# An attention layer in slots of 128 tokens: maxima transposed into the value bank, the latents' softmax normalised behind its product, and the projected queries and keys copied by ScalarE

## The chip, the cores and the metric

The kernel runs on one core of a Trainium2 chip. The metric is the device time of one execution in microseconds. A core has five engines that run their own instruction streams in order and wait for each other by semaphores: TensorE (PE; its weight loads are PEld), VectorE (DVE), ScalarE (ACT), GpSimd (POOL) and SyncE (SP), which here only issues DMA transfers.

## What is computed

The input is x of 4 x 1024 x 256, with a condition of 4 x 256 that gives scales, shifts and gates for each batch. Cut to what matters here:

```
h = layernorm(x) * (1 + scale) + shift
q, k, v = h @ qkv_w                       # 16 heads of 16
local  = softmax(q k^T / 4, keys of the last 128 tokens) @ v
pooled = mean of h over chunks of 16 tokens        # 64 latents
rq = h @ rq_w;  rk, rv = pooled @ rkv_w            # 4 heads of 16
lattn = softmax(rq rk^T / 4, latents of earlier chunks); 0 where there are none
remote = (lattn @ rv) @ rout_w
gate = sigmoid(local @ gl_w + remote @ gr_w)
x1 = x + gated((gate * local + (1 - gate) * remote) @ out_w)
out = a second and a third layernorm of x1, added to x1 by the condition
```

The latents' part is the one whose softmax is changed: for each token and each of 4 heads the exponentials of up to 64 scores, divided by their sum, times the values `rv`.

## The kernel before

The 4096 tokens are 32 tiles of 128 tokens (8 to a batch). Every engine has its program written by hand, as a loop over slots: `slot(t, stages)` does for several tiles one stage each. In slot t the tile t+4 is normalised and transposed, t+3 is projected to queries and keys (`project_half`), t+2 has its queries and keys split into three bf16 terms (`part1`, `res1`, `part2`, `part3`) that SP stores to DRAM and loads again as stacks, t+1 gets its values and latents, t its local scores and their maxima, t-1 its exponentials and their sums with the values, t-2 its gate, mix and output projection, t-3 its last norms. The order in which an engine's `slot` calls its functions is the order on that engine; nothing is reordered afterwards. Semaphores named `..._ready`, `..._psum` or `..._copied` count tiles.

Eight PSUM banks hold everything PE writes, and several stages share each: p_qkv takes the queries and keys of `project_half`, the values of `project_v`, the remote part and the transposed maxima of `max_t`; p_misc takes the latents' product (`lat_out_t`), the transposed outputs (`out_tokens`), the mix and the output projection; p_pv takes the sums of probabilities with values (`sum_v`); p_a takes the transposed input and all of the latents' scores.

The steps of a slot that matter:

- ScalarE's `out_t` copies p_pv to `oT` after the last `sum_v` of the slot before. PE's `max_t` transposes the negated maxima; ScalarE's `shift` spreads them over the heads as 16 extra rows of the stacked queries. Then PE's `scores_t` makes the scores with keys on the partitions, two heads at a time into one of two banks, ScalarE's `exps` takes them out, POOL's `mask` clears what lies outside the window (four heads at a time), and `sum_v` uses them.
- The latents: `lat_scores` (PE), `lat_max` (VectorE), `lat_exp` (ScalarE, four exponentials, each with a sum over the row by the accumulator), `lat_recip` and `lat_norm` (VectorE: `lrec` and `lp`), `lat_p_t` (PE transposes `lp`), `lat_pT` (ScalarE copies it), and in the next slot `lat_out_t` (PE: product with the values spread by head, `bvd`), `lat_oT` (ScalarE copies it to `loT`) and `lat_remote` (PE).
- VectorE's `local_out` makes `local` from `out_tokens`, and POOL's `difference` makes `dif` from it. On POOL a slot is `res1`, `rstd1`, `part3`, `add_u`, `add_bias`, `difference`, `rstd2_of`, three masks, `rstd3_of`, the last mask.
- SP stores the terms of a tile after `part3`; for the odd tile of a pair (its keys) it loads the stack right after that store has landed, in three transfers, and the first scores of the next slot wait for it.

## Time and profile before

| | before |
|---|---|
| median of 3 runs | 580.47 us (572.05, 580.47, 580.49) |
| profiled execution | 576.64 us, span 574.9 us |
| busy, share of the span | PE 482.9 us (84%), VectorE 436.6 (76%), POOL 379.2 (66%), ScalarE 353.8 (62%) |
| weight loads on PE | 364.1 us (63%) |
| mean granted TensorE clock | 0.949 of full |

The span is the time from the first to the last instruction of the profiled execution. Busy times are sums over an engine's instructions. Matmuls overlap each other in the array and their ends are modelled, so a busy PE is not a PE without waits. In rows of the timeline a start, a length, the engine, the line of the kernel and the operation with its output and input stand in that order; in brackets is the idle time of the engine just before, and what ended it.

### The profile page before, as it was taken

To read this page: it belongs to the slowest core of one execution; us is meant where nothing else is said; L and a number is where in the kernel's file an instruction comes from. 1 tells how busy PE (TensorE), PEld (TensorE's weight loads), DVE (VectorE), ACT (ScalarE), POOL (GpSimd) and SP (SyncE) were. 2 spreads that over 40 slices of the span, in tenths; PEclk is the share of its full clock that TensorE was granted. 3 is DMA by queue.
4 is the path that set the end of the run, shared out by engine and by line. 5 is a ranking of instruction groups with operands and counts; after the bars stand their busy time and mean duration, and the time that the engine had idled before them with its cause. 6 is when DMAs were issued, how large, how long until landed. Compare 5 with 4: busy or idle time off the path is not lost.

```text
span 574.9 us, 19855 instructions
## 1 busy us (share of the span) xinstructions
PE 482.9 (84%) x7168; PEld 364.1 (63%) x7168; DVE 436.6 (76%) x1193; ACT 353.8 (62%) x868; POOL 379.2 (66%) x516
## 2 busy tenths in 40 slices
PE   2446689999899999999999999999999999988771
PEld 2205567777677666777777676777776676766451
DVE  2155657788688888988988788888888887878554
ACT  1210466677677667777777577777776776766540
POOL 2222346778577767788877587777777677766663
PEclk9975889999899999999999899999999999999776
DMA  9558644618244444434252607162534444440000
GB/s 277 114 133 246 163 105 99 132 47 187 56 113 75 95 94 93 94 90 93 64 101 68 119 34 145 39 125 62 120 68 97 92 94 93 82 79 10 11 10 19
DMA packets 56523, 55.15 MB, mean 96 GB/s; under 512 B 7380, under 2 KB 53100, under 8 KB 54892
## 3 DMA queue, kind: packets, MB, share of 16 engines
q1 hardware_dynamic: 53564, 52.57, 41.4%
q10 hardware_dynamic: 2864, 1.31, 1.1%
q8 instruction: 59, 0.97, 0.8%
q14 instruction: 36, 0.29, 0.2%
HBM read 37.07 MB, written 16.80 MB: 94 GB/s over the span
## 4 chain that ended last, share of the span: by engine, by line
PE 72%; issue 11%; POOL 5%; DVE 4%; DMA 2%; ACT 2%; ACTq 1%; SPq 1%; POOLq 0%; DVEq 0%
PE p_pv L819 9%; PE p_qkv L730 9%; PE p_qkv L740 6%; PE p_misc L886 6%; PE p_y L806 5%; PE p_x L785 5%; PE p_y L807 5%; PE p_x L778 4%; PE p_a L751 3%; PE p_qkv L860 3%; PE p_misc L869 2%; PE p_a L831 2%; PE p_a L716 2%; PE p_misc L877 2%; PE p_a L753 2%
## 5 line engine op out<-in xcount | busy, mean ns | idle before, releaser
L592 ACT ACTIVATE pr<-p_y 128x512 f32<-128x512 f32 x224 | 124.6, 595 | 55.8 <-PE p_y L807 52.9
L1159 DVE TENSOR_REDUCE mtok<-p_x 128x3 bf16<-128x480 f32 (+1 forms) x192 | 109.3, 585 | 30.9 <-PE p_x L785 29.6
L441 POOL TENSOR_SCALAR_AFFINE_SELECT pr<-pr 128x512 f32<-128x512 f32 x128 | 89.6, 701 | 11.2 <-ACT pr L594 9.0
L451 POOL TENSOR_TENSOR rstd<-ve,half 128x1 f32<-128x1 f32 x96 | 58.1, 605 | 47.9 <-DVE ve L1079 47.7
L469 POOL TENSOR_TENSOR dif<-local,rem 128x272 f32<-128x272 f32 x32 | 30.9, 965 | 83.8 <-DVE local L1197 83.8
L445 POOL TENSOR_SCALAR_AFFINE_SELECT pr<-pr 128x512 f32<-128x512 f32 x112 | 81.3, 726 | 0.0
L807 PE MATMUL p_y<-qst,kst 112*128 112x128 bf16 x512 | 73.2, 221 | 0.0
L806 PE MATMUL p_y<-qst,kst 112*128 112x128 bf16 x448 | 66.5, 221 | 7.7 <-ACT pr L592 4.8
L819 PE MATMUL p_pv<-pr,vp 128*18 128x128 f32 x1920 | 67.1, 279 | 2.1 <-POOL pr L445 0.8
L730 PE MATMUL p_qkv<-hT,wqk 128*128 128x256 f32 x256 | 66.1, 403 | 2.2 <-DVE qkf L1111 1.3
L740 PE MATMUL p_qkv<-wv,hT 128*128 128x272 f32 x128 | 40.1, 439 | 29.5 <-issue 29.4
L819 PEld LDWEIGHTS p_pv<-pr,vp 128*18 128x18 f32 x1920 | 48.0, 99 | 19.8 <-POOL pr L445 10.3
L583 ACT ACTIVATE qst<-p_qkv 16x2048 bf16<-16x2048 bf16 x32 | 59.8, 1869 | 0.8
L785 PE MATMUL p_x<-kst,qst 96*32 96x160 bf16 x1792 | 59.3, 235 | 0.5 <-issue 0.5
L600 ACT ACTIVATE oT<-p_pv 128x512 f32<-128x512 f32 x32 | 19.1, 597 | 65.6 <-PE p_pv L819 65.6
L807 PEld LDWEIGHTS p_y<-qst,kst 112*128 112x128 bf16 x512 | 49.0, 99 | 9.7 <-issue 0.9
L730 PEld LDWEIGHTS p_qkv<-hT,wqk 128*128 128x128 f32 x256 | 48.3, 199 | 9.3 <-issue 2.2
L806 PEld LDWEIGHTS p_y<-qst,kst 112*128 112x128 bf16 x448 | 42.8, 98 | 17.5 <-issue 7.9
L425 POOL TENSOR_TENSOR qkf<-qkf,terms 128x512 f32<-128x512 f32 x32 | 40.7, 1271 | 19.5 <-ACT terms L571 19.4
L740 PEld LDWEIGHTS p_qkv<-wv,hT 128*128 128x128 f32 x128 | 23.2, 201 | 37.6 <-issue 34.7
L778 PE MATMUL p_x<-edge,ident_bf 128*32 128x192 bf16 (+1 forms) x672 | 43.5, 249 | 4.0 <-issue 3.9
L432 POOL TENSOR_TENSOR terms<-qkf,terms 128x512 bf16<-128x512 f32 x32 | 37.1, 1160 | 11.7 <-ACT terms L577 11.6
(131 smaller groups left out, 1092.7 us busy)
## 6 DMA issues: line engine op xcount, KB each, us to landing
scr_q<-terms SPq DMA_DIRECT2D x16, 384.0 KB, 2.5
qst<-scr_q SPq DMA_DIRECT2D x16, 384.0 KB, 4.7
scr_k<-terms SPq DMA_DIRECT2D x16, 384.0 KB, 4.4
kst<-scr_k SPq DMA_DIRECT2D x16, 384.0 KB, 5.4
qst<-scr_q SPq DMA_DIRECT2D x16, 256.0 KB, 5.4
kst<-scr_k SPq DMA_DIRECT2D x16, 256.0 KB, 6.4
out_y<-y SPq DMA_DIRECT2D x32, 128.0 KB, 1.7
x_all<-in_x SPq DMA_DIRECT2D x3, 1024.0 KB, 8.3
```

The source lines that it names most:

```text
L441: ins = pool.affine_select(out=own, in_=own, compare_op=ALU.is_ge, fill=0.0, base=-1, pattern=[[0, 4], [1, P]], channel_multiplier=-1)
L445: ins = pool.affine_select(out=prev, in_=prev, compare_op=ALU.is_ge, fill=0.0, base=-1, pattern=[[0, 4], [-P, P]], channel_multiplier=P + 1)
L583: act.activation(q_of(t)[KS:KS + H, :, :], p_qkv[KS:KS + H, 0:P // 2].bitcast(BF16).unsqueeze(1).to_broadcast([H, H, P]), ACT.Copy).then_i ...
L592: act.activation(pr[:, 2 * i:2 * i + 2, :, :], src, ACT.Exp).then_inc(exp_done[i], 1)
L730: ins = pe.matmul(p_qkv[:, 2 * b * P:2 * (b + 1) * P], wqk[:, k, half * D + b * P:half * D + (b + 1) * P], hT[:, r:r + 2, k, :], start=(k ...
L740: ins = pe.matmul(p_qkv[:, 0:H * (HD + 1)], hT[:, t % 4, k, :], wv[:, k, :, :].rearrange("p h k -> p (h k)"), start=(k == 0), stop=(k == K ...
L778: pe.matmul(ends[g * QG:(g + 1) * QG], ident_bf[:, g * QG:(g + 1) * QG], edge[:, :].unsqueeze(1).to_broadcast([P, h1 - h0, 2 * QG]).rearra ...
L785: ins = pe.matmul(win[g * QG:(g + 1) * QG, h - h0, :], q_of(t)[0:KS, h, g * QG:(g + 1) * QG], keys[:, at:at + WIN], start=False, stop=True ...
L806: pe.matmul(p_y[i % 2][:, at:at + P], kst[0:KS + H, h, (n - 1) % NB, :], q, start=True, stop=True)
L807: ins = pe.matmul(p_y[i % 2][:, at + P:at + 2 * P], kst[0:KS + H, h, n % NB, :], q, start=True, stop=True)
L819: ins = pe.matmul(p_pv[32 * j:32 * j + VC, g * P:(g + 1) * P], vp[:, (n - 1 + a) % RING, h, :], pr[:, h, a, :], start=(a == 0 or n % NB == ...
L1159: dve.tensor_reduce(mtok[:, KS + h0:KS + h1], p_x[i % 2][:, 0:(h1 - h0) * w].rearrange("p (h n) -> p h n", n=w), AX_X, ALU.max, negate=Tru ...
```

## The change

Three edits go together.

1. `max_t` writes the transposed maxima into p_pv instead of p_qkv, and `shift` reads them there. So `project_v` waits for the remote part of an earlier tile instead of `shift`, and `max_t` waits for `oT` of the tile before. On PE `scores(t, 1)` is now ahead of `max_t`.
2. The latents' exponentials are transposed and multiplied as they are, without sums by the accumulator. The constant 0/1 pattern of `bvd` stands beside the values, so that the same product gives 64 rows of values and 64 rows of the sums, each repeated for its head's 16 rows. VectorE then takes the reciprocal of the sums (`rden`, 64x128) and multiplies (`loT`); ScalarE's copy `lat_oT` is gone. For the first tile of a batch the 16 tokens without latents are set to 0 from `rden`.
3. `copy_qk` moves from VectorE (one operation of 128x512) to ScalarE (two of 128x256), between the exponentials 4 and 7 of the slot. In ScalarE's slot `out_t` now comes before `part1`, and `shift` before `part2`.

```diff
             def shift(t):
                 act.wait_ge(mT_psum, done(t))
                 act.wait_ge(st_psum[LAST_ST], done(t - 4))
-                act.activation(q_of(t)[KS:KS + H, :, :], p_qkv[KS:KS + H, 0:P // 2].bitcast(BF16).unsqueeze(1).to_broadcast([H, H, P]),
+                act.activation(q_of(t)[KS:KS + H, :, :], p_pv[KS:KS + H, 0:P // 2].bitcast(BF16).unsqueeze(1).to_broadcast([H, H, P]),
                                ACT.Copy).then_inc(shift_ready, 1)
...
+            def copy_qk(t):
+
+                half = t % 2
+                act.wait_ge(qk_psum, done(t))
+                act.wait_ge(part3_ready, done(t - 2))
+                for b in range(KC):
+                    ins = act.activation(qkf[:, half, b, :], p_qkv[:, 2 * b * P:2 * (b + 1) * P], ACT.Identity,
+                                         bias=bqk[:, half, b:b + 1])
+                ins.then_inc(qk_copied, 1)
...
             def project_v(t):
                 pe.wait_ge(hT_ready, done(t))

-                pe.wait_ge(shift_ready, done(t - 2))
+                pe.wait_ge(rem_ready, done(t - 3))
                 pe.wait_ge(qk_copied, done(t + 1))
...
             def max_t(t):
                 pe.wait_ge(s_max[LAST_MAX], done(t))

-                pe.wait_ge(qk_copied, done(t + 3))
-                pe.wait_ge(rem_ready, done(t - 1))
-                pe.transpose(p_qkv[:, 0:P // 2].bitcast(BF16), mtok[:, :], ident_bf[:, :]).then_inc(mT_psum, 1)
+                pe.wait_ge(oT_ready, done(t - 1))
+                pe.transpose(p_pv[:, 0:P // 2].bitcast(BF16), mtok[:, :], ident_bf[:, :]).then_inc(mT_psum, 1)
...
             def lat_exp(t):
                 act.wait_ge(lmx_ready, done(t))
-                act.wait_ge(lp_ready, done(t - 1))
+                act.wait_ge(lpT_psum, done(t - 1))
                 for h in range(LH):
-                    ins = act.activation(by_head(le, t)[:, h, :], by_head(p_a, t)[:, h, :], ACT.Exp, bias=lneg[:, h:h + 1],
-                                         accum_out=lsum[:, h:h + 1])
+                    ins = act.activation(by_head(le, t)[:, h, :], by_head(p_a, t)[:, h, :], ACT.Exp, bias=lneg[:, h:h + 1])
...
-            def lat_oT(t):
-                act.wait_ge(loT_psum, done(t))
-                act.wait_ge(rem_psum, done(t - 1))
-                act.activation(loT[0:LD, :], p_misc[0:LD, 0:P], ACT.Copy).then_inc(loT_ready, 1)
...
             def lat_recip(t):
-                dve.wait_ge(lexp_ready, done(t))
+
+                dve.wait_ge(loT_psum, done(t))
+                dve.reciprocal(rden[:, :], p_misc[LD:2 * LD, 0:P]).then_inc(rden_ready, 1)
+
+            def lat_norm(t):
+
+                dve.wait_ge(rden_ready, done(t))
+                dve.wait_ge(rem_psum, done(t - 1))
                 if t % NB:
-                    dve.reciprocal(lrec[:, :], lsum[:, :]).then_inc(lval_ready, 1)
+                    dve.tensor_tensor(loT[0:LD, :], p_misc[0:LD, 0:P], rden[:, :], ALU.mult).then_inc(loT_ready, 1)
...
```

Where the three edits move rows: on ScalarE, between the end of one slot and the start of the next (`mixT`, `lpT` close a slot; `terms` are `part1` and `part2`, `oT` is `out_t`, `qst` is `shift`), before:

```order
L638 ACTIVATE mixT<-p_misc 128x256 [waits out_psum,mixT_psum]
L615 ACTIVATE lpT<-p_a 128x256 [waits loT_psum,lpT_psum]
L571 ACTIVATE terms<-qkf 128x512 [waits q_terms_stored,qk_copied]
L600 ACTIVATE oT<-p_pv 128x512 [waits o_psum,pv_psum0]
L577 ACTIVATE terms<-qkf 128x512 [waits res_ready]
L583 ACTIVATE qst<-p_qkv 16x16x128 [waits st_psum6,mT_psum]
L620 ACTIVATE loT<-p_misc 64x128 [waits rem_psum,loT_psum]
```

and after:

```order
L642 ACTIVATE mixT<-p_misc 128x256 [waits out_psum,mixT_psum]
L624 ACTIVATE lpT<-p_a 128x256 [waits loT_psum,lpT_psum]
L610 ACTIVATE oT<-p_pv 128x512 [waits o_psum,pv_psum0]
L581 ACTIVATE terms<-qkf 128x512 [waits k_terms_stored,qk_copied]
L593 ACTIVATE qst<-p_pv 16x16x128 [waits st_psum6,mT_psum]
L587 ACTIVATE terms<-qkf 128x512 [waits res_ready]
L617 ACTIVATE le<-p_a,lneg 128x64 [waits lpT_psum,lmx_ready]
```

`part1` went from the end of the slot to behind `oT`, `part2` from ahead of `shift` to behind it, and the copy to `loT` is gone.

On VectorE, from `norm1` (`xn`) to `local` of one slot, before:

```order
L1094 TENSOR_SCALAR xn<-x_all,mv,rstd 128x256 [waits hT_psum,rstd1_ready]
L1159 TENSOR_REDUCE mtok<-p_x 128x3 [waits mT_psum,s_psum3]
L1118 TENSOR_TENSOR vp<-p_qkv,bv 128x16x17 [waits pv_psum0,v_psum]
L1186 TENSOR_SCALAR ssum<-p_misc 128x16 [waits o_psum]
L1064 BN_AGGR mv<-st 128x2 [waits st2_ready]
L1191 RECIPROCAL srec<-ssum 128x16 [waits ssum_ready]
L1079 TENSOR_SCALAR ve<-mv 128x1 [waits mv2_ready]
L1197 TENSOR_TENSOR local<-p_misc,srec 128x272 [waits dif_ready,srec_ready]
```

and after:

```order
L1106 TENSOR_SCALAR xn<-x_all,mv,rstd 128x256 [waits hT_psum,rstd1_ready]
L1175 RECIPROCAL rden<-p_misc 64x128 [waits loT_psum]
L1182 TENSOR_TENSOR loT<-p_misc,rden 64x128 [waits rem_psum,rden_ready]
L1163 TENSOR_REDUCE mtok<-p_x 128x3 [waits mT_psum,s_psum3]
L1122 TENSOR_TENSOR vp<-p_qkv,bv 128x16x17 [waits pv_psum0,v_psum]
L1191 TENSOR_SCALAR ssum<-p_misc 128x16 [waits o_psum]
L1076 BN_AGGR mv<-st 128x2 [waits st2_ready]
L1196 RECIPROCAL srec<-ssum 128x16 [waits ssum_ready]
L1091 TENSOR_SCALAR ve<-mv 128x1 [waits mv2_ready]
L1202 TENSOR_TENSOR local<-p_misc,srec 128x272 [waits dif_ready,srec_ready]
```

The reciprocal `rden` and the product `loT` now stand between `norm1` and the maxima, so ahead of `vp`, `ssum` and `local`.

On PE, at the start of an even slot (the first with a new pair's stacks), before:

```order
L795 MATMUL p_qkv<-ident_bf,mtok 128x128 [waits rem_ready,qk_copied,s_max4]
L778 MATMUL p_x<-edge,ident_bf 32x3x2x32 [waits s_max5,k_stack_loaded,q_stack_loaded]
L778 MATMUL p_x<-edge,ident_bf 32x3x2x32 x3
L785 MATMUL p_x<-kst,qst 32x160 x12
L778 MATMUL p_x<-edge,ident_bf 32x3x2x32 [waits s_max4,k_stack_loaded,q_stack_loaded]
```

and after:

```order
L788 MATMUL p_x<-edge,ident_bf 32x3x2x32 [waits s_max5,k_stack_loaded,q_stack_loaded]
L788 MATMUL p_x<-edge,ident_bf 32x3x2x32 x3
L795 MATMUL p_x<-kst,qst 32x160 x12
L804 MATMUL p_pv<-ident_bf,mtok 128x128 [waits oT_ready,s_max4]
L788 MATMUL p_x<-edge,ident_bf 32x3x2x32 [waits s_max4,k_stack_loaded,q_stack_loaded]
```

The transpose of `mtok` went behind the first scores, into p_pv, and waits for `oT`.

## Rows read from the trace of the kernel before

**Rows 1.** Who waited for whom, 82.1 to 558.4 us (us in total, times, longest)
```profile
POOL dif L469 <- DVE local L1197: 81.8, 31, 5.6
...
PEld p_qkv L740 <- issue: 32.3, 29, 1.4
```

**Rows 2.** The chain that ended last, 280 to 330 us (start, us, what)
```profile
284.15 0.16 PE p_qkv L795
...
285.02 0.63 PE p_a L831 x2
...
288.71 0.44 PE p_misc L869 x4
...
293.35 1.81 PE p_qkv L730 x8
...
298.13 1.44 PE p_pv L819 x48
```

**Rows 3.** Timeline of ScalarE, 269 to 300 us
```profile
284.22 0.60 ACT L600 ACTIVATE oT<-p_pv 128x512 f32<-128x512 f32 x1 [1.85 <-PE p_pv L819]
284.71 0.62 ACT L577 ACTIVATE terms<-qkf 128x512 bf16<-128x512 f32 x1
285.36 1.87 ACT L583 ACTIVATE qst<-p_qkv 16x2048 bf16<-16x2048 bf16 x1
...
295.42 1.09 ACT L592 ACTIVATE pr<-p_y 128x512 f32<-128x512 f32 x2 [1.17 <-PE p_y L807]
...
297.09 0.63 ACT L571 ACTIVATE terms<-qkf 128x512 bf16<-128x512 f32 x1
```

**Rows 4.** Timeline of POOL, 269 to 300 us
```profile
284.58 0.56 POOL L451 TENSOR_TENSOR rstd<-ve,half 128x1 f32<-128x1 f32 x1 [0.78 <-DVE ve L1079]
...
290.21 1.00 POOL L469 TENSOR_TENSOR dif<-local,rem 128x272 f32<-128x272 f32 x1 [2.22 <-DVE local L1197]
...
297.83 1.32 POOL L425 TENSOR_TENSOR qkf<-qkf,terms 128x512 f32<-128x512 f32 x1
```

**Rows 5.** Timeline of VectorE, 269 to 300 us
```profile
286.59 0.82 DVE L1094 TENSOR_SCALAR xn<-x_all,mv,rstd 128x256 f32<-128x256 f32 x1
287.33 0.65 DVE L1159 TENSOR_REDUCE mtok<-p_x 128x3 bf16<-128x480 f32 x1
288.52 0.44 DVE L1118 TENSOR_TENSOR vp<-p_qkv,bv 128x272 f32<-128x272 f32 x1 [0.55 <-PE p_qkv L740]
289.19 0.17 DVE L1186 TENSOR_SCALAR ssum<-p_misc 128x16 f32<-128x16 f32 x1 [0.23 <-PE p_misc L869]
...
289.69 0.44 DVE L1197 TENSOR_TENSOR local<-p_misc,srec 128x272 f32<-128x272 f32 x1
```

**Rows 6.** Line of the oT copies: count, ns, first and last start
```profile
L600 ACT ACTIVATE oT<-p_pv x32: 597/597/597, 82.1 to 558.3; 128x512 f32<-128x512 f32 x32
```

**Rows 7.** Groups by form (count, busy us, mean ns, idle before)
```profile
L638 ACT ACTIVATE mixT<-p_misc 128x256 f32<-128x256 f32 x32 | 12.3, 383 | 8.4 <-PE p_misc L877 7.9
...
L1125 DVE TENSOR_SCALAR rqT<-p_a,brq 64x128 f32<-64x128 f32 x32 | 10.4, 326 | 1.8 <-PE p_a L756 1.8
...
L1191 DVE RECIPROCAL srec<-ssum 128x16 f32<-128x16 f32 x32 | 8.1, 253 | 0.0
...
L1171 DVE RECIPROCAL lrec<-lsum 128x4 f32<-128x4 f32 x28 | 4.7, 168 | 0.0
...
L984 DVE RECIPROCAL cs<-cs 128x8 f32<-128x8 f32 x1 | 0.2, 203 | 0.0
```

**Rows 8.** Timeline of the DMA queue, 284 to 300 us
```profile
286.59 0.38 SPq L350 DMA_DIRECT2D scr_k<-terms  x1
```

**Rows 9.** The line of the stack reloads, 290 to 294 us
```profile
L370 SPq DMA_DIRECT2D kst<-scr_k x3: 557/619/640, 291.3 to 292.6; - x3
...
DMA to landing us min/median/max: 5.4/6.3/6.5
```

**Rows 10.** Busy times of 318 to 322 us; granted clock third from the end
```profile
318.00:322.00 4.00, 4.00 (x31) 2.96 (x32) 1.42 (x8) 1.87 (x11) 0.51 (x1) 0.58 0.40 111
```

More of the change, by code:

```diff
@@ L647, in slot @@
                 if Q:
-                    part2(r)
+                    part1(r)
                 if T:
                     shift(m)
-                    lat_oT(m)
+                if Q:
+                    part2(r)
                 if S:
@@ L667, in slot @@
                     exps(m, 4)
+                if PR:
+                    copy_qk(h)
+                if T:
                     exps(m, 7)
@@ L679, in _ @@
             modulated(b1)
+            copy_qk(b0)
             part1(b0)
+            copy_qk(b1)
             part2(b0)
@@ L850, in lat_out_t @@
                 for k in range(chunks):
-                    ins = pe.matmul(p_misc[:, 0:P], bvd[:, t % 2, k, :], lpT[:, k * P:(k + 1) * P],
+                    ins = pe.matmul(p_misc[:, 0:P], values_of(t)[:, k, :], lpT[:, k * P:(k + 1) * P],
                                     start=(k == 0), stop=(k == chunks - 1))
@@ L893, in slot @@
                 A, PR, K, S, T, C = ("A" in stages, "P" in stages, "K" in stages, "S" in stages, "T" in stages, "C" in stages)
+                if S:
+                    scores(t, 1)
                 if T:
@@ L896, in slot @@
                 if S:
-                    scores(t, 1)
                     scores(t, 0)
@@ L1023, in weights @@
                       dve.memset(loT[LD:LD + 1, :], 1.0),
+                      *[dve.tensor_copy(bvd[:, r, :, LD:2 * LD], cst[:, C_RV:C_RV + 2 * LD].rearrange("p (k l) -> p k l", k=2))
+                        for r in range(2)],
+                      *[dve.tensor_copy(bvd1[:, r, LD:2 * LD], cst[:, C_RV1:C_RV1 + LD]) for r in range(2)],
                       dve.tensor_copy(rqT[LD:P, 0, :], cst[LD:P, C_IND:C_IND + P]),
@@ L1104, in pool_tokens @@
                                   AX_X, ALU.add).then_inc(pooled_ready, 1)
-            def copy_qk(t):
-                half = t % 2
-                dve.wait_ge(qk_psum, done(t))
-                dve.wait_ge(part3_ready, done(t - 2))
-                dve.tensor_tensor(qkf[:, half, :, :], p_qkv[:, :].rearrange("p (b n) -> p b n", b=KC),
-                                  bc(bqk[:, half, :], 2 * P), ALU.add).then_inc(qk_copied, 1)
             def copy_v(t):
@@ L1270, in slot @@
                     norm1(a)
+                if T:
+                    lat_recip(m)
+                    lat_norm(m)
                 if S:
```

55 lines of the change are left out of this document (18 added, 37 removed).

## The prediction

> **What bounds the kernel now.** I began with the table of who waited for whom [rows 1]. Its longest lines have an engine standing still before the same few events of every slot: POOL before `dif`, 81.8 us in 31 slots, and PE before `project_v`, 32.3 us in 29. The second is the wait that this change removes: `project_v` writes p_qkv, and ScalarE's `shift` still reads it. Whether that wait sets the end is a question for the slot, so I next took one full slot and laid its four engines beside each other: PE by the chain that ended last [rows 2], ScalarE [rows 3], POOL [rows 4], VectorE [rows 5]. All times below are of that slot (t = 15), which begins for PE at 284.15 and for the next tile at 299.57; the 32 `oT` copies, 82.1 to 558.3 us [rows 6], give (558.3 - 82.1) / 31 = 15.36 us for a slot.
>
> The reader is to see two things. First, PE's chain of waits looks like a PE bound (nearly every piece of it is a matmul), but the slot closes on POOL. `dif` starts at 290.21, 0.08 after VectorE's `local` ends (289.69 + 0.44), and from there POOL runs without a pause (the ten rows left out there, eight selects in four masks among them, carry no idle time in brackets) to the residual that follows the last mask at 297.83 [rows 4]; PE's last 48 sum matmuls start at 298.13 [rows 2], and their end starts the next slot. So whatever delays `local` delays the slot by the same amount. Second, ScalarE ends the slot nearly as late: its last pair of exponentials starts at 295.42 [rows 3], the moment PE is past `project_half`, and mask 3 follows that pair. Both chains arrive together; neither has room for half a microsecond.
>
> **The change part by part.**
>
> *Maxima in the value bank.* `project_v` no longer waits for `shift`: it gives PE up to 32.3 / 29 = 1.1 us per slot. But the transpose of the maxima now waits for `oT` (284.22 + 0.60 = 284.82 [rows 3]), where it ran at 284.15 [rows 2]; `scores(t, 1)`, put ahead of it, fills 0.4 of that, so 0.3 of idle PE comes back, and `scores(t, 0)`, the latents' scores and their values' product are queued behind it and start 0.3 later than at 285.02 [rows 2]. `shift` itself starts no earlier: ScalarE has `oT` and `part1` in front of it, 0.49 + 0.65, which is again 285.36 [rows 3]. Net for PE alone: a gain of 0.8 per slot at `project_v`.
>
> *ScalarE's new order.* `part1` ran in the idle time before `oT` (297.09 [rows 3]; the residual on POOL started right behind the mask at 297.83 [rows 4]). Now it stands behind `oT`, which waits for the end of the sums. That is no cost to ScalarE, but POOL's next two instructions are the residual `res1` and then the `rstd` that VectorE's `norm1` needs. So: `part1` 284.71 to 285.34, `res1` of 1.32 [rows 4] to 286.74, `rstd` of 0.56 [rows 4] to 287.30, `norm1` at about 287.35, where the trace has it at 286.59 [rows 5]. That is 0.75 late. `part2`, the third term and the store to DRAM move with it; I come back to them.
>
> *Latents normalised behind the product.* VectorE loses a reciprocal of 128x4 (0.17), the product `lp` and, with the next part, the copy of 128x512: more than a microsecond, but all of it behind `local`, where VectorE isn't what the slot waits for. It gains a reciprocal of 64x128 and a product of 64x128, and these stand between `norm1` and the next maxima, ahead of `local`. No reciprocal of that width is in the trace. From below, an ordinary operation of 64x128 out of PSUM takes 0.33 [rows 7]. From above, reciprocals take 168 ns at 4 elements, 203 at 8 and 253 at 16 [rows 7], 6 to 9 ns more per element: 0.253 + 112 x 0.0062 to 0.253 + 112 x 0.0088, which is 0.95 to 1.23. I take 1.05 (the 7.1 ns between 4 and 16), because the three rows are of the same operation. 
> The chain then reads: `norm1` 287.35, reciprocal 288.09 (the step of 0.74 that now leads from `norm1` to the maxima [rows 5]) to 289.14, product of 0.33 (the same row as the lower bound) to 289.5. Two things wait for it. PE's `out_tokens` needs `loT` out of p_misc: 289.55 instead of 288.71 [rows 2], 0.84 late, with the 0.8 gained at `project_v` spent standing there. VectorE's maxima of 0.65 and `copy_v` of 0.44 follow (1.0 together with their overlap), and `local` starts 0.50 after the sums (289.19 to 289.69) [rows 5]: 289.45 + 1.0 + 0.5, about 290.9 instead of 289.69. So `dif`, and with it mask 3 and the slot's end, are 1.2 late.
>
> ScalarE's `loT` copy and the four reads of the accumulator go. This is hidden either way: the exponentials that follow wait for `scores_t`, and the second of them now stands behind `out_tokens`.
>
> *Copy of queries and keys on ScalarE.* Two operations of 128x256; the nearest row is 0.383 for 128x256 out of p_misc [rows 7], so 0.66 to 0.77 for both. They wait for `project_half` and stand ahead of the last two exponentials. In the trace ScalarE is idle before these (they start at 295.42), since their scores are queued behind `project_half`, which PE leaves at 293.35 + 1.81 = 295.16 [rows 2]; the copy can't use that idle time, since it waits for the same matmuls. `project_half` 0.84 late plus 0.4 (0.66 less the 0.26 from 295.16 to 295.42, in which those scores run) makes the last exponentials 1.2 to 1.3 late: the same as POOL's path. Were the cover gone on one side, the other would still hold the slot; so the two are not added.
>
> *The store and reload of keys.* The third term ended right before its store at 286.59 [rows 8]. Now `part2` comes after `shift` (285.36 + 1.87 = 287.23), and the third term ends some 2.5 later. The last of the three reloads was issued at 292.6 and took 6.5 [rows 9], so it landed at 299.1, 0.5 before 299.57, where the next slot's scores need it. With 2.5 more it lands at 301.6, while the new slot would start at 300.8: 0.8 to 1.0 late in every second slot (the keys' ones). Of this 0.3 hides in the wait for `oT`, and some 0.4 in `norm1`'s wait for `rstd`, which starts from `oT` and isn't moved by it. 0.2 is left, up to 0.5.
>
> *Set-up.* Four more copies of 128x128 and 128x64 on VectorE against three of 128x512 that leave it for ScalarE: I count nothing.
>
> **Sum.** 1.2 in one slot and 1.4 in the other, mean 1.3, in 31 slots [rows 6]: 40 us. On the profiled execution's own 576.64 that is 617 us. The median of the three runs shown lies 3.8 higher and the lowest 4.6 lower, so I leave the sum on its own execution. A change below 2%, some 12 us, can't be told from none here.
>
> **The rivals.**
>
> *A cheap reciprocal.* At 0.33 instead of 1.05 the chain to `local` is only 0.5 late, and ScalarE's path 0.1 + 0.45. That is 0.55 x 31 = 17 us: 594. For it: the row of 0.33 is of the same shape; against it: three reciprocal rows of one slope.
>
> *The clock falls more often.* The granted clock is at its full 2.4 GHz in most of the trace, but in 318 to 322, after a wait of PE, the row shows a mean of 0.58 [rows 10], so for most of that stretch the lower level, 1.2 GHz: 4 x 0.42 = 1.7 us of work lost. PE will now stand still at two places of a slot instead of one. If every second slot pays it, 16 x 1.7 = 27 us more: 644. Against it: a wait of 1.1 stands in 29 slots now [rows 1], and the mean clock of the whole run is still 0.949 of full (the table above).
>
> *Faster: PE is the bound after all.* If the slot's length came from PE's own sequence, and the tail on POOL and ScalarE had room, `project_v`'s 1.1 less the 0.3 at the transpose would be kept: 0.85 x 31 = 26 us, 550 us. It decides at `dif`: it would have to start no later than 290.21 - 284.15 = 6.06 after the slot's begin. For it speaks PE's busy share, the highest in the table above, and its chain of waits; against it POOL's unbroken run from `dif` to the last mask.
>
> *No difference.* If `res1` were early after all or slack that I don't see took the delays, gains and losses would cancel: 570 to 590.
>
> **How the numbers follow.** Forecast 617 (605 to 632 with the bounds of reciprocal and reload): 0.63. Cheap reciprocal 0.15, half of it within 2%. Clock 0.08. Faster 0.07. No difference 0.07. Faster by over 2%: 0.07; within 2%: 0.07 + 0.07 = 0.14; slower: 0.63 + 0.08 + 0.08 = 0.79. The range takes in the forecast's own and the cheap reciprocal: 593 to 636; the faster case and most of the clock's are left out.
>
> **What would show it.** In the profile after: `project_v` without idle time before it; a reciprocal of 64x128 near 1.05 us; `rstd` for `norm1` 3.1 us after the start of `oT`; PE idle before `out_tokens`; `local` about 6.7 us after `oT` starts, where it is 5.5 now; POOL still unbroken from `dif` to the last mask; `oT` every 16.6 us. A reciprocal of a third of a microsecond, or a pause on POOL between `dif` and the last mask, would prove the sum wrong.

## The result and the profile after

| | before | after |
|---|---|---|
| median, lowest to highest | 578.85 us (572.05 to 580.49) | 602.3 us (598.28 to 609.28) |
| profiled execution, its span | 576.64, 574.9 us | 604.86, 603.1 us |
| busy: PE, VectorE, ScalarE, POOL | 482.9, 436.6, 353.8, 379.2 us | 489.9, 433.3, 357.4, 374.6 us |
| mean granted clock | 0.949 | 0.947 |

The ratio of the times is 1.04, 95% interval 1.0292 to 1.0507: slower, by 28.2 us of span (603.1 - 574.9). The ratio leaves out the run of 609.28, which counts as slow, and takes in a fifth run of 599.67. Busy times moved by 7 us at most and the mean clock by 0.002, so the time went into waits.

The page of the profile after: the chain by engine, the new copy's group (busy us, mean ns, idle before it), and the keys' store (issues, KB each, us to landing).

```profile
PE 60%; issue 15%; ACT 8%; POOL 6%; DMA 4%; DVE 4%; ACTq 1%; SPq 1%; POOLq 0%; DVEq 0%
...
L572 ACT ACTIVATE qkf<-p_qkv,bqk 128x256 f32<-128x256 f32 x64 | 26.9, 471 | 44.4 <-PE p_qkv L740 44.4
...
scr_k<-terms SPq DMA_DIRECT2D x16, 384.0 KB, 2.5
```

Who waited for whom after, over the whole span (us in total, times, longest):

```profile
POOL qkf L425 <- ACT terms L581: 95.4, 31, 9.0
...
ACT qkf L572 <- PE p_qkv L740: 44.4, 32, 6.4
...
DVE mtok L1163 <- PE p_pv L804: 33.9, 30, 3.1
PEld p_misc L877 <- issue: 29.7, 30, 1.8
POOL terms L432 <- ACT terms L587: 29.1, 31, 2.3
POOL dif L469 <- DVE local L1202: 28.7, 27, 7.3
...
POOL pr L441 <- ACT pr L604: 16.9, 13, 2.7
...
POOL pr L441 <- ACT pr L602: 11.6, 25, 1.6
```

`project_v`'s wait [rows 1] is no longer there: edit 1 does what it says. In its place weights stand still before `out_tokens` (29.7 us, 30 times), 1.0 a slot. POOL now waits for `part1` at the head of a slot (95.4), for `part2` (29.1), and before masks for exponentials (11.6, and 16.9 in the first tiles of the batches); its wait for `local` is 28.7, where it was 81.8 in 31 slots [rows 1].

The reciprocal and `oT` by line (count, ns min/median/max, first and last start):

```profile
L1175 DVE RECIPROCAL rden<-p_misc x32: 958/959/961, 70.4 to 572.8; 64x128 f32<-64x128 f32 x32
```
```profile
L610 ACT ACTIVATE oT<-p_pv x32: 597/598/599, 82.7 to 586.9; 128x512 f32<-128x512 f32 x32
```

A slot is (586.9 - 82.7) / 31 = 16.26 us, where it was 15.36 [rows 6]: 0.90 more in 31 slots is the 28. The slot t = 15 after runs from `oT` at 295.65 to the next at 311.82. ScalarE's timeline in it:

```profile
295.65 0.60 ACT L610 ACTIVATE oT<-p_pv 128x512 f32<-128x512 f32 x1 [2.41 <-PE p_pv L828]
296.15 0.62 ACT L581 ACTIVATE terms<-qkf 128x512 bf16<-128x512 f32 x1
...
307.05 0.84 ACT L572 ACTIVATE qkf<-p_qkv,bqk 128x256 f32<-128x256 f32 x2 [0.92 <-PE p_qkv L740]
307.78 1.09 ACT L602 ACTIVATE pr<-p_y 128x512 f32<-128x512 f32 x2
308.74 0.41 ACT L642 ACTIVATE mixT<-p_misc 128x256 f32<-128x256 f32 x1
```

VectorE's, which has `local` at 5.97 after `oT` (301.62 - 295.65; before, 289.69 - 284.22 = 5.47 [rows 3, 5]):

```profile
296.72 0.66 DVE L1163 TENSOR_REDUCE mtok<-p_x 128x3 bf16<-128x480 f32 x1 [0.85 <-PE p_pv L804]
...
298.59 0.41 DVE L1106 TENSOR_SCALAR xn<-x_all,mv,rstd 128x256 f32<-128x256 f32 x1
299.02 0.96 DVE L1175 RECIPROCAL rden<-p_misc 64x128 f32<-64x128 f32 x1
300.02 0.28 DVE L1182 TENSOR_TENSOR loT<-p_misc,rden 64x128 f32<-64x128 f32 x1
...
301.62 0.44 DVE L1202 TENSOR_TENSOR local<-p_misc,srec 128x272 f32<-128x272 f32 x1
```

And POOL's, with a pause of 0.57 before the last mask that wasn't there before:

```profile
296.85 1.16 POOL L425 TENSOR_TENSOR qkf<-qkf,terms 128x512 f32<-128x512 f32 x1 [2.86 <-ACT terms L581]
...
302.14 0.93 POOL L469 TENSOR_TENSOR dif<-local,rem 128x272 f32<-128x272 f32 x1 [0.19 <-DVE local L1202]
...
308.94 0.64 POOL L441 TENSOR_SCALAR_AFFINE_SELECT pr<-pr 128x512 f32<-128x512 f32 x1 [0.57 <-ACT pr L602]
```

The chain that ended last names what closes the slot (start, us, what): PE's wait before `out_tokens` (0.56), then `project_half`, ScalarE's copy (from 307.05, above), the exponentials behind it, `mixT`, the output projection, the sums. Between `out_tokens` and `project_half` PE waits for next to nothing.

```profile
299.84 0.56 issue
300.40 0.63 PE p_misc L877 x4
...
305.23 1.80 PE p_qkv L740 x8
...
307.78 0.64 ACT pr L602 x2
...
308.74 0.41 ACT mixT L642
...
309.19 1.13 PE p_misc L894 x4
310.32 1.48 PE p_pv L828 x48
```

### The profile page after: what moved, and what is told of

It is laid out like the page before. It is cut to its first block, busy times and chain, and to the rows that moved or that the text cites. A ratio compares the mean times of both kernels' runs of the same rounds, so it can differ in the third digit from the quotient of the medians.

```text
span 603.1 us, 19694 instructions
## 1 busy us (share of the span) xinstructions
PE 489.9 (81%) x7168; PEld 367.7 (61%) x7168; DVE 433.3 (72%) x1165; ACT 357.4 (59%) x772; POOL 374.6 (62%) x516
## 4 chain that ended last, share of the span: by engine, by line
PE 60%; issue 15%; ACT 8%; POOL 6%; DMA 4%; DVE 4%; ACTq 1%; SPq 1%; POOLq 0%; DVEq 0%
PE p_qkv L740 9%; PE p_pv L828 7%; PE p_misc L894 5%; PE p_qkv L750 5%; PE p_y L815 4%; PE p_y L816 3%; PE p_x L795 3%; PE p_x L788 3%; PE p_misc L877 3%; PE p_a L761 3%; ACT pr L602 3%; ACT oT L610 3%; PE p_qkv L868 2%; PE p_a L840 2%; PE p_a L763 2%
## 5 line engine op out<-in xcount | busy, mean ns | idle before, releaser
L441 POOL TENSOR_SCALAR_AFFINE_SELECT pr<-pr 128x512 f32<-128x512 f32 x128 | 86.8, 678 | 28.6 <-ACT pr L604 16.9
L425 POOL TENSOR_TENSOR qkf<-qkf,terms 128x512 f32<-128x512 f32 x32 | 37.0, 1156 | 95.4 <-ACT terms L581 95.4
L445 POOL TENSOR_SCALAR_AFFINE_SELECT pr<-pr 128x512 f32<-128x512 f32 x112 | 88.9, 794 | 0.0
L451 POOL TENSOR_TENSOR rstd<-ve,half 128x1 f32<-128x1 f32 x96 | 54.5, 568 | 24.1 <-DVE ve L1091 24.0
L593 ACT ACTIVATE qst<-p_pv 16x2048 bf16<-16x2048 bf16 x32 | 59.9, 1871 | 4.5 <-PE p_pv L804 3.8
L795 PE MATMUL p_x<-kst,qst 96*32 96x160 bf16 x1792 | 62.0, 234 | 0.6 <-issue 0.6
L432 POOL TENSOR_TENSOR terms<-qkf,terms 128x512 bf16<-128x512 f32 x32 | 37.0, 1157 | 29.1 <-ACT terms L587 29.1
L572 ACT ACTIVATE qkf<-p_qkv,bqk 128x256 f32<-128x256 f32 x64 | 26.9, 471 | 44.4 <-PE p_qkv L740 44.4
L469 POOL TENSOR_TENSOR dif<-local,rem 128x272 f32<-128x272 f32 x32 | 29.8, 931 | 29.1 <-DVE local L1202 28.7
L894 PE MATMUL p_misc<-wo,mixT 128*128 128x256 f32 x128 | 39.0, 430 | 9.9 <-ACT mixT L642 9.9
```

The source lines that it names most:

```text
L441: ins = pool.affine_select(out=own, in_=own, compare_op=ALU.is_ge, fill=0.0, base=-1, pattern=[[0, 4], [1, P]], channel_multiplier=-1)
L445: ins = pool.affine_select(out=prev, in_=prev, compare_op=ALU.is_ge, fill=0.0, base=-1, pattern=[[0, 4], [-P, P]], channel_multiplier=P + 1)
L593: act.activation(q_of(t)[KS:KS + H, :, :], p_pv[KS:KS + H, 0:P // 2].bitcast(BF16).unsqueeze(1).to_broadcast([H, H, P]), ACT.Copy).then_in ...
L795: ins = pe.matmul(win[g * QG:(g + 1) * QG, h - h0, :], q_of(t)[0:KS, h, g * QG:(g + 1) * QG], keys[:, at:at + WIN], start=False, stop=True ...
L894: ins = pe.matmul(p_misc[:, 0:D], mixT[:, k * P:(k + 1) * P], wo[:, (t // NB * KC + k) * D:(t // NB * KC + k + 1) * D], start=(k == 0), st ...
```

## The experiments

All slots below are read off the timelines in the same way: the times of an operation after the slot's `oT` starts, and from one `oT` to the next, median over the slots between 150 and 560 us, some 25 of them. The slots of a kernel fall into clusters, so these medians can move by 0.1 with the slots at the ends of the stretch.

| us after `oT` | before | after | maxima_alone | maxima_early_q | early_q_act_copy |
|---|---|---|---|---|---|
| first maxima start | 0.55 | 1.07 | 1.07 | 1.07 | 1.06 |
| `norm1` starts | 2.36 | 2.91 | 2.93 | 2.64 | 2.60 |
| `out_tokens` starts | 4.33 | 4.75 | 4.02 | 3.70 | 3.59 |
| `local` starts | 5.47 | 5.97 | 5.16 | 4.89 | 4.88 |
| `project_half` ends | 10.91 | 11.36 | 10.60 | 10.24 | 10.18 |
| last exponentials end | 12.26 | 13.21 | 11.53 | 11.52 | 12.02 |
| last mask ends | 13.59 | 14.52 | 13.36 | 12.93 | 13.32 |
| next `oT` | 15.34 | 16.18 | 15.08 | 14.91 | 15.07 |

The expectations name theories by letters. After the result there were two: R, the prediction's chain over VectorE and POOL, and T, the tail of the slot, where the last exponentials stand behind ScalarE's copy. After the single undoings and edit 1 alone my theory was P: three chains end a slot side by side (ScalarE's copy before the last exponentials; VectorE's reciprocal before `out_tokens` and `local`; on POOL `part2` behind `shift`, which sets the earliest `dif` by way of the third term), so that taking one away gives little. Its rival is S: the costs of the edits add up. Where a kernel below has 0.05 in place of the reciprocal, the latents' part isn't divided by its sums; nothing else of the work is left out.

**One part undone at a time.** The copy back on VectorE, in its old place:

```diff
                     exps(m, 4)
-                if PR:
-                    copy_qk(h)
```

> The changed kernel with the copy of queries and keys back on VectorE, at its old place; everything else as changed. Theory T (the tail): the slot ends late because the last two exponentials stand behind the copy, which waits for project_half; taking the copy away lets them start about 0.5 earlier after the start of oT (11.6 instead of 12.1), 31 x 0.5 = 15 us, so about 587. Theory R (as recorded): VectorE's chain from norm1 over the reciprocal to local, and POOL behind it, sets the end; the copy is only an equal second path, and nothing is gained: about 602.

Measured: 597.24 us (593.95 to 598.38), ratio to before 1.0377 (1.0321 to 1.0434), slot 15.84. That lies between the two expectations. The last exponentials end at 12.70 in place of 13.21, so 0.51 earlier, while `local` stays at 5.96 and `project_half` ends where it did (11.36).

`part1` ahead of `oT` again:

```diff
-                if C:
-                    out_t(c)
                 if Q:
                     part1(r)
+                if C:
+                    out_t(c)
```

> The changed kernel with part1 ahead of oT again, in ScalarE's idle time at the end of a slot. Theory R: res1 and rstd run early, norm1 starts some 0.75 earlier and the whole chain with it: 31 x 0.75 = 23 us, about 579. Theory T: norm1 is held as much by the maxima, which wait for the transpose behind oT (it starts at once after the maxima in most slots), so 0 to 0.2 per slot, 596 to 602.

Measured: 596.93 us (594.69 to 597.67), ratio 1.0375 (1.0323 to 1.0426), slot 15.94. This is T's number. `norm1` starts only 0.2 to 0.3 earlier (2.6 to 2.7), since the maxima ahead of it on VectorE hold it too, and `local` not at all (5.97). The slots lie in two clusters, at 15.83 and 16.17, and the median between them.

The reciprocal replaced by a product with a constant, of the same shape:

```diff
-                dve.reciprocal(rden[:, :], p_misc[LD:2 * LD, 0:P]).then_inc(rden_ready, 1)
+                dve.tensor_scalar(rden[:, :], p_misc[LD:2 * LD, 0:P], 0.05, None, ALU.mult).then_inc(rden_ready, 1)
```

> The changed kernel with the reciprocal of 64x128 replaced by a multiplication with a constant of the same shape: the division by the latents' sums is left out. It gives the price of the reciprocal on the path: its 0.96 becomes about 0.33, out_tokens then waits for PE's own work and starts about 0.55 earlier. Theory T: 31 x 0.55 = 17 us, about 585. Theory R: 31 x 0.63 = 20 us, about 583. If the reciprocal were hidden: 602.

Measured: 594.4 us (591.69 to 597.71), ratio 1.034 (1.0278 to 1.0402), slot 15.65. Both expectations had 583 to 585. `local` is 0.68 earlier (5.29), `out_tokens` 0.67 (4.08), `project_half` ends 0.67 earlier (10.69) and the last exponentials 0.68 (12.53): the division delays them one for one. Of the slot's 0.84 the division is 0.53, but the time doesn't show it. In four slots it takes 17.8 to 21.5 us, since PE waits for a late stack of keys:

```profile
216.29 0.35 PE L788 MATMUL p_x<-edge,ident_bf 128*32 128x192 bf16 x4 [3.86 <-issue]
```

Over the whole run such waits are these (us, times, longest), here and in the changed kernel:

```profile
PE p_x L788 <- issue: 13.6, 6, 4.0
```
```profile
PE p_x L788 <- issue: 3.9, 3, 1.4
```

In the traces every one of these waits at the start of an even slot ends 0.09 after the last of the three reloads has landed.

Each of the three intervals overlaps that of the whole change, so by time alone no single undoing can be told from none; their slots can (0.34, 0.24 and 0.53 shorter).

**Two undone, then all three.** The constant and the copy on VectorE (ScalarE's new order stays):

```diff
-                if PR:
-                    copy_qk(h)
...
-                dve.reciprocal(rden[:, :], p_misc[LD:2 * LD, 0:P]).then_inc(rden_ready, 1)
+                dve.tensor_scalar(rden[:, :], p_misc[LD:2 * LD, 0:P], 0.05, None, ALU.mult).then_inc(rden_ready, 1)
```

> The changed kernel with two undone: the copy of queries and keys back on VectorE, and the reciprocal replaced by a multiplication with a constant of the same shape (the division by the latents' sums is left out). What stays is ScalarE's order with part1 behind oT and part2 behind shift. Theory P (three chains end side by side, each alone nearly enough): POOL can't start dif before its part3, add_u and add_bias are through, 6.2 after the start of oT, and its masks take 7.6 from there, so the slot stays at 15.5 to 15.6 and the time at 583 to 588, little under the 594 of the divide alone. Theory S (the costs add: 0.34 and 0.53 per slot): 15.3 per slot, 575.

Measured: 588.2 us (587.48 to 589.08), ratio 1.0185 (1.0134 to 1.0235), slot 15.49, at the edge of what P had. The last exponentials end at 12.02, 1.19 earlier than in the changed kernel: the 0.51 of the copy and the 0.68 of the division, added. POOL's timeline of a slot (`oT` at 291.51):

```profile
292.71 1.16 POOL L425 TENSOR_TENSOR qkf<-qkf,terms 128x512 f32<-128x512 f32 x1 [2.94 <-ACT terms L571]
...
295.25 1.16 POOL L432 TENSOR_TENSOR terms<-qkf,terms 128x512 bf16<-128x512 f32 x1 [0.87 <-ACT terms L577]
...
297.06 0.73 POOL L478 TENSOR_TENSOR xb<-x_all,obg 128x256 f32<-128x256 f32 x1
297.75 0.95 POOL L469 TENSOR_TENSOR dif<-local,rem 128x272 f32<-128x272 f32 x1
```

`dif` has no idle time before it: `local` was done at 297.25 (296.81 + 0.44), and `dif` started 0.5 later, behind the third term that waits for `part2`. This is the third chain, and ScalarE's order alone makes it: with the order undone too (below), `dif` starts 0.28 earlier, and the slot is 0.10 shorter.

The copy on VectorE and ScalarE's old order (the division stays):

```diff
+                if Q:
+                    part1(r)
                 if C:
                     out_t(c)
                 if Q:
-                    part1(r)
+                    part2(r)
                 if T:
                     shift(m)
-                if Q:
-                    part2(r)
...
-                if PR:
-                    copy_qk(h)
```

> The changed kernel with the copy back on VectorE and ScalarE's order as before (part1, oT, part2, shift); the latents' division behind the product stays. Theory P: the reciprocal still makes out_tokens and local late, the slot stays at 15.6 to 15.8 and the time at 588 to 595, almost that of the copy alone (597). Theory S (0.34 and 0.24 or more add up): 15.55 or less, 584.

Measured: 594.22 us (589.89 to 595.29), ratio 1.0264 (1.0191 to 1.0336), slot 15.79, with `local` at 6.07 and `project_half` ending at 11.56: the reciprocal by itself, within P's range.

The constant and ScalarE's old order (the copy stays on ScalarE):

```diff
+                if Q:
+                    part1(r)
                 if C:
                     out_t(c)
                 if Q:
-                    part1(r)
+                    part2(r)
                 if T:
                     shift(m)
-                if Q:
-                    part2(r)
...
-                dve.reciprocal(rden[:, :], p_misc[LD:2 * LD, 0:P]).then_inc(rden_ready, 1)
+                dve.tensor_scalar(rden[:, :], p_misc[LD:2 * LD, 0:P], 0.05, None, ALU.mult).then_inc(rden_ready, 1)
```

> The changed kernel with ScalarE's order as before and the reciprocal replaced by a multiplication with a constant of the same shape (the division is left out); the copy of queries and keys stays on ScalarE. Theory P: the copy's chain alone holds the slot, the last exponentials end 12.5 after the start of oT as without the divide alone, slot 15.5 to 15.65, about that of the divide alone (15.65). Theory S (0.53 and 0.24 add): 15.4 or less. In microseconds the late keys' stacks of single slots blur it, 585 to 594.

Measured: 581.93 us (581.61 to 583.9), ratio 1.0122 (1.0097 to 1.0147), slot 15.50: the slot in the place that P expected, the time below it. By time the copy alone is the cheapest of the three.

All three undone, which leaves edit 1 and the product with the sums in it:

```diff
+                if Q:
+                    part1(r)
                 if C:
                     out_t(c)
                 if Q:
-                    part1(r)
+                    part2(r)
                 if T:
                     shift(m)
-                if Q:
-                    part2(r)
...
-                if PR:
-                    copy_qk(h)
...
-                dve.reciprocal(rden[:, :], p_misc[LD:2 * LD, 0:P]).then_inc(rden_ready, 1)
+                dve.tensor_scalar(rden[:, :], p_misc[LD:2 * LD, 0:P], 0.05, None, ALU.mult).then_inc(rden_ready, 1)
```

> The changed kernel with all three undone: the copy on VectorE, ScalarE's order as before, the reciprocal replaced by a constant factor (the division is left out). What stays is the first edit and the latents' product with its sums beside it. Theory P: with the last of the three chains gone, POOL starts dif at about 5.7 and not 6.24, and the slot falls to that of the first edit alone, 15.1, from 15.5 with two undone. If the remaining parts of the change cost something, it stays at 15.3 or more. The late keys' stacks come back with the short slot, so 572 to 580 us in all.

Measured: 579.65 us (577.41 to 581.62), ratio 1.006 (1.0016 to 1.0105). Its median slot of 15.39 is longer than P's 15.1; the expectation took 15.3 or more to mean that the rest of the change costs something.

With these, every combination of the three has a ratio. The last column is PE's waits before scores that no engine's work ends (the lines `PE p_x <- issue` of who waited for whom, added up), most of them for stacks:

| division | new order | copy on ScalarE | ratio to before | slot | waits for stacks, us |
|---|---|---|---|---|---|
| no | no | no | 1.006 | 15.39 | 7.9 |
| no | no | yes | 1.0122 | 15.50 | 3.2 |
| no | yes | no | 1.0185 | 15.49 | 15.3 |
| yes | no | no | 1.0264 | 15.79 | 6.3 |
| no | yes | yes | 1.034 | 15.65 | 13.6 |
| yes | no | yes | 1.0375 | 15.94 | 5.0 |
| yes | yes | no | 1.0377 | 15.84 | 9.3 |
| yes | yes | yes | 1.04 | 16.18 | 4.5 |

Each put on alone adds 0.6% (copy), 1.25% (order), 2.0% (division), 3.9% together; the whole adds 3.4%, with an interval of more than 1% to either side. So the ratios don't exclude costs that add up, and what blurs them is the last column. With these waits taken off the medians (an estimate, since they are of one execution each), copy, order and division alone add 7.0, 1.2 and 16.2 us, together 24.3, and the whole 26.0; each pair comes within 3 of its sum.

The slots agree. Alone the three add 0.11, 0.10 and 0.40, together 0.61, and the whole 0.79. If the longest of chains side by side set the slot, the whole would be as long as the dearest part alone, 15.79, and not 16.18. So P doesn't hold for the whole change, and S does within 0.2 a slot, though not with the numbers that the expectations gave it, which came from the single undoings. The reason is in the rows: division and copy stand one behind the other on one chain, `out_tokens`, `project_half`, the copy, the last exponentials. The order costs little in the slot; of the 8.6 us that it adds alone (588.2 - 579.65), 7.4 are more waits for stacks.

**Edit 1 alone.** The kernel before with the transposed maxima in p_pv and the order on PE that goes with them:

```diff
-                pe.wait_ge(shift_ready, done(t - 2))
+                pe.wait_ge(rem_ready, done(t - 3))
...
-                pe.transpose(p_qkv[:, 0:P // 2].bitcast(BF16), mtok[:, :], ident_bf[:, :]).then_inc(mT_psum, 1)
+                pe.wait_ge(oT_ready, done(t - 1))
+                pe.transpose(p_pv[:, 0:P // 2].bitcast(BF16), mtok[:, :], ident_bf[:, :]).then_inc(mT_psum, 1)
```

> The kernel before with the first edit alone: maxima transposed into the value bank, the order of PE as changed, ScalarE's and VectorE's order as before. Theory T: VectorE's first maxima now wait for the transpose behind oT (0.5 later), but project_v no longer waits for shift, so local and out_tokens come about 0.3 earlier: 31 x 0.3 = 9 us less than before, about 569. Rival: the wait for oT costs as much as the one removed, 575 to 582. By R's count of PE alone, 0.8 per slot, it would be 554.

Measured: 577.27 us (575.26 to 583.83), ratio 1.0051 (1.0014 to 1.0089): no gain, although the median slot is 0.26 shorter. Four slots take 18.2 to 19.4 us, where before has one over 18 (18.72). One of them in the chain that ended last:

```profile
208.55 2.42 issue
210.97 0.27 PE p_x L778 x4
...
213.64 2.11 PE p_qkv L740 x4
```

PE stands 2.42 before the first scores with a new pair's stacks; the reload of the keys was issued at 203.16. The granted clock behind that wait (third number from the end):

```profile
208.00:212.00 4.00, 1.57 (x55) 0.99 (x46) 1.73 (x7) 1.47 (x3) 2.88 (x5) 1.00 0.57 85
212.00:216.00 4.00, 4.00 (x34) 2.87 (x31) 2.38 (x6) 2.85 (x10) 0.68 (x1) 0.57 0.29 102
```

It is 0.57 in 212 to 216, so most of that stretch is at the lower level of 1.2 GHz, and `project_v` takes 2.11 there, 1.11 in the slot before (at 197.92). The last of the three reloads landed 0.09 before PE went on. A shorter slot leaves the reload less time, and a late stack costs twice.

**The order on the DMA queue.** Edit 1 alone, and in even slots the queries' stack is loaded ahead of the store of the output, so that its reads are out of the way sooner:

```diff
-                if Q and t % 2:
+                if Q:
                     load_stack(r)
                 if D_:
                     store(d)
-                if Q and t % 2 == 0:
-                    load_stack(r)
```

> The kernel before with the first edit alone, and on SP the reload of the queries' stack ahead of the store of the output in even slots (about 2 us earlier), so that it is out of the way of the next slot's store of the keys' terms. In the run without this, slots were 15.08 instead of 15.34, but PE waited for late keys' stacks in some slots, up to 2.4 us, and those slots took 18 to 19. If these stalls are what gave the first edit's gain back: the keys' stack lands a microsecond or two earlier, no slot over 17 but those with the load of a batch, about 562 to 567. If not: 576.

Measured: 561.65 us (560.06 to 565.41), ratio 0.9734 (0.9674 to 0.9794), slot 14.91. It is faster than both kernels. The keys' stores land in 2.8 us in the median (2.5 to 5.3), with edit 1 alone in 5.2 (3.5 to 7.4).

The same order in the kernel before, as a control:

```diff
-                if Q and t % 2:
+                if Q:
                     load_stack(r)
                 if D_:
                     store(d)
-                if Q and t % 2 == 0:
-                    load_stack(r)
```

> Control: the kernel before with only that order on SP. Its slots are 15.34, with one long slot (18.7) that waited for the keys' stack: at most 3 us to gain, 572 to 576.

Measured: 572.92 us (570.03 to 578.7), ratio 0.9929 (0.9885 to 0.9972), slot 15.29: a small part of it. With the stack in time, edit 1 takes the ratio from 0.9929 to 0.9734; without, from 1 to 1.0051.

The same order in the changed kernel:

```diff
-                if Q and t % 2:
+                if Q:
                     load_stack(r)
                 if D_:
                     store(d)
-                if Q and t % 2 == 0:
-                    load_stack(r)
```

> The changed kernel with the queries' stack loaded ahead of the store of the output in even slots, nothing else. Theory: in the changed kernel the keys' stack is not late (its stores land in 2.5 us and no slot waits for it), so the order on the queue changes nothing of the slot's 16.18: 596 to 606 us. Rival, the late third term puts the key reload on the path in every second slot: as with edit 1 alone, where the same order took 15 us off: 585 to 592 us.

Measured: 600.14 us (598.61 to 603.33), ratio 1.0454 (1.0406 to 1.0501), slot 16.15. Nothing changes. The expectation's reason isn't quite right: PE waits for a stack in three even slots of the changed kernel (3.9 us, above) and in five with this order (5.6 us, longest 2.5). But in most slots the late third term puts no reload on the path.

**ScalarE's copy on the best kernel.** Edit 1 with the early stack, and the copy on ScalarE, nothing else:

```diff
                     exps(m, 4)
+                if PR:
+                    copy_qk(h)
+                if T:
                     exps(m, 7)
                     exps(m, 6)
```

> The kernel with edit 1 and the earlier loading of queries (561.65 us, slot 14.91 in the median, last exponentials over 11.52 after oT), plus the copy of queries and keys on ScalarE between exponentials 4 and 7, and nothing else of edits 2 and 3. Theory of chains that end side by side: the last pair of exponentials ends 1.66 to 1.85 after project_half (so it did with the copy on ScalarE, 12.55 - 10.89 and 13.21 - 11.36), which is 10.24 + 1.75 = 12.0 in place of 11.52; all of the 0.4 to 0.6 shows in the slot because nothing else ends as late: slot 15.3 to 15.5, 573 to 582 us. Rival, the edits' costs add up: the copy costs what its single undoing gave, 5 us: slot about 15.05, 565 to 568 us.

Measured: 570.49 us (568.22 to 572.63), ratio 0.993 (0.99 to 0.996), against 0.9734 without the copy: between the two expectations. The last exponentials end at 12.02, just where the theory put them, 0.50 later; but the slot lengthens by 0.41 only where it is widest (15.49 for 15.08), and by 0.16 in the median. The theory's "nothing else ends as late" was wrong. The end of a slot in the chain of the kernel without the copy:

```profile
300.70 1.78 PE p_qkv L728 x8
...
303.40 0.44 PE p_misc L873 x2
303.84 0.56 PE p_pv L816 x16
304.40 1.06 PE p_misc L882 x4
305.46 1.48 PE p_pv L816 x48
306.94 0.02 issue
```

From `project_half` to the end PE waits for next to nothing, so PE bounds this part of the slot. It doesn't bound all of the kernel: earlier in the same slot some 6 us of ScalarE lie in the chain (`oT` at 292.57 to 298.60), and in the next slot `mixT`. With the copy, ScalarE's waits stand in the chain between `project_half` and `mixT`, and the 16 sums (0.56) that lay in it are no longer there. I take it that they run in that wait instead, which would cover part of the 0.50; no run shows it by itself.

## Why the prediction was right, and where its sizes were off

Direction and range held; the sum was too large by 12 (40 forecast, 28 measured). Of the two chains that were to end the slot, the one put first, over `local` and POOL, doesn't end it, and the one named beside it does. That both had been given the same 1.2 kept the number near, which was luck.

*`project_v`'s wait goes, and the gain is spent at `out_tokens`:* right. The wait is gone, and the weights of `out_tokens` stand 1.0 a slot. Edit 1 alone shows it unspent: `out_tokens` at 4.02 in place of 4.33.

*`part1` behind `oT` delays `norm1` by 0.75:* measured 0.55 (2.36 to 2.91). `res1` took 1.16 and not 1.32, so `rstd` ends at 298.53. But I missed a second cause of the same size: the first maxima write the tile that the transpose reads, so they wait for it, and it now waits for `oT` (0.55 to 1.07). The maxima ahead of `norm1` end at 298.67. That is why undoing the order alone gave 0.2 to 0.3.

*Reciprocal 1.05, product 0.33, `norm1` to reciprocal 0.74:* measured 0.96, 0.28 and 0.43. The step was the largest error of this part. I took it from a slot in which POOL's additions run beside `norm1` ([rows 5], and POOL's row at the end); after, POOL waits for `part2` at that time, and the operation takes 0.41 in all 24 slots between 100 and 480 us. So `out_tokens` is 0.42 late and `local` 0.50, where I had 0.84 and 1.2. The Trainium skill ("SBUF — State Buffer", section "Who interferes with whom") says that a `tensor_scalar` of VectorE can hold a port pair that it shares with GpSimd, and that the one that issues later then waits; the two traces agree (below). By the Trainium skill's page that the prediction cites ("VectorE: DVE Perf Modes", section "First, the fixed hardware budget"), the estimate was 1.07, 0.11 above what was measured. The slope of the narrow reciprocals [rows 7] was also high, (959 - 253) / 112 = 6.3 ns an element.

*POOL runs unbroken from `dif` to the last mask, and this ends the slot:* the step that failed. POOL waits 0.57 before the last mask here, 11.6 us in 25 waits. I had said that such a pause would prove the sum wrong, and it does so for the chain that I led it along, not for the one named beside it. The reading was wrong for before too. There the chain that ended last is PE's alone from `project_v` (287.33) to the end of the sums, and POOL's last mask ended at 297.86, 0.27 before the last sums started, while PE was at the output projection (POOL's row, then PE's chain):

```profile
297.23 0.63 POOL L445 TENSOR_SCALAR_AFFINE_SELECT pr<-pr 128x512 f32<-128x512 f32 x1
```
```profile
297.07 1.06 PE p_misc L886 x4
298.13 1.44 PE p_pv L819 x48
```

In the whole run of before PE's sums wait for a mask three times, 1.5 us in all. So a later `local` didn't delay the slot by the same amount: before there was room, and after `local` is 0.50 late and the last mask 0.93, held by the exponentials.

*ScalarE's copy ahead of the last exponentials, 1.2 to 1.3 late:* the chain that does end the slot. In the medians `project_half` ends 0.45 later (forecast 0.84) and the exponentials end 1.85 behind it where it was 1.35, so 0.50 more for the copy (forecast 0.4; the pair takes 0.84, forecast 0.66 to 0.77). Together 0.95, and the slot is 0.84 longer in the median, 0.90 in the mean.

*Two chains aren't added:* right for the sum, since 0.50 and 0.95 would be 1.45 and the slot is 0.84 longer. That one would hold the slot were the other's cover gone is not what the runs show: without the copy it loses 0.34, without the division 0.53. The delay that the division gives to `project_half` and the copy lie on the same chain, and there they add. The third chain, `part2` behind `shift` on POOL, I used for the reload alone; it holds `dif` at 6.24 when reciprocal and copy are gone.

*The reload of keys late by 0.2 in even slots:* didn't occur in most. The third term does end 2.55 later (4.90 after `oT` in place of 2.35; forecast 2.5). The store was issued at 300.58, but landed in 2.5 us. The reload left at 303.14, 7.49 after `oT`, where the first of its three left at 291.3 [rows 9], 7.1 after `oT` [rows 3]; and the longer slot gives it more time. In three even slots PE does wait for it, up to 1.4. Where the slot is shorter, without the division, the term is real: 13.6 us of waits, most of what the order costs in time.

*The rivals.* The cheap reciprocal is out (0.96). The clock gave no more away over the whole run (0.947, before 0.949). But what the rival described is there in the last slot of each of the first three batches, where PE stands 1.7 before `out_tokens`. In one of them, from `oT` at 327.7 (granted clock third from the end):

```profile
333.70:335.70 2.00, 2.00 (x29) 1.16 (x32) 1.33 (x7) 1.20 (x3) 1.23 (x3) 0.61 0.49 173
335.70:337.70 2.00, 2.00 (x23) 1.75 (x19) 1.46 (x4) 0.97 (x4) 1.27 (x3) 0.54 0.50 131
```

All three take 16.5. With the other queue order two of them keep the full clock behind the same wait and take 15.0 and 15.1, and the one at 0.66 and 0.50 takes 16.5: such a fall costs 1.4 to 1.5. PE as the bound, which I had start from `dif` at 6.06 or earlier, is out for the whole change (6.49), but describes the end of a slot with edit 1 and the stack in time: `dif` at 5.41 in the kernel of 561.65 us, where PE runs from `project_half` to the end.

What stays open: why the median slot with all three undone (15.39) is 0.31 above that of edit 1 alone, though their times are alike (what is left of edit 2 is one place to look: `out_tokens` starts at 4.22 there and not 4.02, `project_half` ends at 10.90 and not 10.60); why the whole adds 0.18 a slot more than its three parts; and what the remaining 0.5% of edit 1 alone over before would be without its late stacks, beyond what the control gives.

## What to carry to other kernels

When undoing one of several edits shows nothing in the time, look at the slot before the edit is called free: here each undoing took 0.24 to 0.53 off the slot, and waits elsewhere hid it. Undo pairs and put each on alone, and ask whether the parts stand side by side (then the longest counts) or one behind the other (then they add). A wait that is removed early in a slot is a gain only if what runs on a fixed delay (here a store and a reload through DRAM) can follow; look at it first when the typical slot is shorter and the total isn't. When the cost of a step is taken from a timeline, look at what ran on the other engines beside it, and ask whether it will still run there.

## What was not expected of the hardware

- `norm1`, a `tensor_scalar` of 128x256 in SBUF, takes 0.41 us with nothing on POOL and 0.47 to 0.90 beside POOL's `tensor_tensor`. Before, 23 of 24 slots between 100 and 480 us have such an instruction beside it and one has not; in the 23, `norm1` ends about 0.15 after a POOL instruction that was running beside it. VectorE's rows:

```profile
150.29 0.41 DVE L1094 TENSOR_SCALAR xn<-x_all,mv,rstd 128x256 f32<-128x256 f32 x1
165.46 0.82 DVE L1094 TENSOR_SCALAR xn<-x_all,mv,rstd 128x256 f32<-128x256 f32 x1
```

POOL's, in the slot of [rows 5], where `norm1` runs from 286.59 to 287.41:

```profile
286.53 0.73 POOL L484 TENSOR_TENSOR ux<-x,b 128x256 f32<-128x256 f32 x1
```

- The same store of the keys' terms, 384 KB, lands in 2.5 us in the median of after, 4.4 in that of before (2.8 to 7.7) and 5.2 with edit 1 alone. What makes it slow wasn't measured by itself, but the order of loads on one queue was worth 15.6 us there (577.27 to 561.65).
